# Self-attention of a decoder layer: mask and maxima in one VectorE instruction per head and row half

## The chip, the cores and the metric

The kernel runs on one core of one Trainium2 chip. The metric is the device time of one execution in microseconds (us). The core has a matrix engine (TensorE, PE in the profile, with its weight loads shown as PEld), a vector engine (VectorE, DVE), an activation engine (ScalarE, ACT), a general engine (GpSimd, POOL) and a queue engine (SyncE, SP), which all run their own instruction streams and wait for each other by semaphores.

## What is computed

One decoder layer on x of shape (16, 224, 512): causal self-attention with 16 heads of 32 channels, cross-attention to a context of 750 rows, and a gated recurrence with an output gate, each followed by a residual sum and a layer norm. Only the first of the three stages changes:

```python
def _L0_attn_ref(x, Wq, Wk, Wv, Wu, bu):          # h = 16 heads, c = 32
    xh = x.reshape(b, t, h, c)
    scale = d ** (-0.25)
    q = jnp.einsum('bthc,oc->btho', xh, Wq) * scale
    k = jnp.einsum('bthc,oc->btho', xh, Wk) * scale
    v = jnp.einsum('bthc,oc->btho', xh, Wv)
    scores = jnp.einsum('bihc,bjhc->bhij', q, k)
    scores = jnp.where(j > i, -jnp.inf, scores)
    attn = jax.nn.softmax(scores, axis=-1)
    y = jnp.einsum('bhij,bjhc->bihc', attn, v).reshape(b, t, d)
    return y @ Wu.T + bu
x = _layernorm(x + _L0_attn_ref(x, ...), axis=-1)
```

## The kernel before

Self-attention goes through 64 steps: step n is batch n // 4 and group g = n % 4 of four heads (G = 4). The 224 rows of a batch are two halves of R = 112 rows; the upper half (index 1, buffer `p1`, 224 columns) sees all columns up to its own, the lower half (index 0, buffer `p0`, 112 columns) only the first 112. Scores of head h stand in PSUM bank h (`ps_s`), first the upper half's 224 columns, then the lower half's 112. There is one set of these four banks, so the scores of step n+1 overwrite those of step n. The probabilities `p0` and `p1` have four buffers, one for each g.

The work is software-pipelined by hand: each engine has a function `steps` that lists, for step n, what it does for steps n, n-1, n-2, n-3 and n-4. An engine executes its list in order, so the order around the change is this.

- TensorE (`tensor`, L231 to L442), step n: `s(n)` the scores (L261), `t(n-2, 1)` a transposition of four 112x112 blocks (L292), `pv(n-3)` the products with the rows of x (L304, L307), `t(n-2, 2)`, `t(n-1, 0)`, in even steps `z` (the projected columns of a coming step, L243 to L247), and between them the pieces of the output projection `w` (L321), one of 128x512 each: seven in an odd step, five in an even one.
- ScalarE (`scalar`), step n: `exp(n)` for heads 0 and 1, `exp(n)` for heads 2 and 3 (L459; with the row sums through an accumulator, so each exponential is two instructions), `yh(n-3)` (L469) between or after them, `pt_copy(n-2)` (L485), and in even steps `open_projection` (L478) and `z_copy` (L492).
- VectorE (`vector`), step n: `inverse(n-1)` (the reciprocal of the row sums, L578), in even steps `yl(n-4)` (L591), `smax(n)` for heads 0 and 1 (L569 and L570: the negated maximum of the upper half and of the lower half), `pt_copy(n-2, 1)` (L585), `smax(n)` for heads 2 and 3, in even steps `yl(n-3)`, `norm` (L622) and `residual` (L599), in odd ones `statistics` (L605), in every fourth `moments` (L613, L615), and last `pt_copy(n-1, 0)` (L585).
- GpSimd (`gpsimd`), step n: `normalise(n-1)`, which multiplies `p1` and then `p0` by the reciprocals (L757), and in odd steps `query_parts` (L744, L746) for a coming `z`.

The causal mask is added by TensorE. `mask` is a bf16 tile of 0 and -1e30 for two identical triangles; one product of it with the bf16 identity (224 columns) puts it on the last 112 columns of the upper half and on the 112 columns of the lower half of one head. For heads 0 to 2 these products (L268) stand ahead of the score products and open the bank, each as soon as ScalarE has taken the exponentials of the same head of the step before; for head 3 it stands behind them (L279). The score products are L272 (224 columns) and L275 (112 columns). They wait until all exponentials of the step before are taken (`exp_done`), since ScalarE reads the scores in PSUM. `smax` waits for each head (`s_done`).

## Time and profile before

| | |
|---|---|
| median of 3 runs | 1409.38 us |
| the 3 runs | 1409.38, 4735.66, 1404.38 us |
| the profiled execution | 1403.68 us |
| its span (first to last instruction) | 1401.7 us |
| mean granted TensorE clock | 0.997 |
| self-attention in that span | from 0 to some 377 us |

The profile is one execution. Busy time is the union of an engine's instruction records; the records of neighbouring instructions overlap by some hundredths of a us, so the time that an instruction takes of its engine is read from the start of one to the start of the next. TensorE's records overlap more. [...]

### The profile page before, as it was taken

The numbers are of one execution on the slowest core, as the hardware profiler recorded it, in microseconds if no ns is written. First come the engines' busy times: TensorE is split into PE (matmuls) and PEld (weight loads), VectorE is DVE, ScalarE is ACT, GpSimd is POOL, SyncE is SP. The second block draws the span as 40 slices with busy tenths as digits, with TensorE's granted clock in tenths as the row PEclk, the third lists the DMA queues.
The fourth block names the chain that finished last, engine by engine and source line by source line (L and its number), as shares of the span: only waits on it lengthen the run. The fifth ranks groups of instructions, "written<-read, shape, count | busy, mean of one in ns | idle before, by whom it ended". The sixth has DMA issues, their size and how long they took to land.

```text
span 1401.7 us, 28348 instructions
## 1 busy us (share of the span) xinstructions
PE 1370.4 (98%) x9969; PEld 1203.7 (86%) x9969; DVE 862.9 (62%) x1911; ACT 731.7 (52%) x2005; POOL 574.7 (41%) x475
## 2 busy tenths in 40 slices
PE   7999999999989999999999999999999999999997
PEld 3677777777789999999999888999999999999775
DVE  4589989999745555654664372445443454536697
ACT  4588888888565566566656454222222222322232
POOL 2567767676556665656566520000000000010264
PEclk9999999999999999999999999999999999999999
DMA  6114323336288899889999963011010100000363
GB/s 215 38 44 107 105 77 80 105 103 170 80 216 184 215 221 218 188 220 210 208 199 226 214 177 102 0 27 27 0 26 0 26 13 20 31 1 31 105 188 121
DMA packets 141651, 159.07 MB, mean 113 GB/s; under 512 B 70400, under 2 KB 78592, under 8 KB 141568
## 3 DMA queue, kind: packets, MB, share of 16 engines
q1 hardware_dynamic: 133888, 157.96, 44.7%
q10 hardware_dynamic: 7680, 0.03, 0.4%
q8 instruction: 49, 0.80, 0.3%
q14 instruction: 34, 0.28, 0.1%
HBM read 106.57 MB, written 35.80 MB: 102 GB/s over the span
## 4 chain that ended last, share of the span: by engine, by line
PE 63%; issue 3%; DMA 3%; POOL 2%; DVE 1%; ACT 1%; POOLq 0%; SPq 0%; ACTq 0%; DVEq 0%
PE banks L1603 16%; PE banks L1632 11%; PE banks L1040 9%; PE banks L1056 8%; PE banks L1634 6%; PE banks L1025 5%; PE banks L1072 5%; DMA s_x1t<-x_halves 1%; POOL o_r L2178 1%; PE banks L1010 1%; PE banks L2064 1%; DMA x_halves<-s_ahead_halves 1%; PE banks L1088 1%; POOL o_rstd L2186 1%; PE banks L2095 0%
## 5 line engine op out<-in xcount | busy, mean ns | idle before, releaser
L459 ACT ACTIVATE s_p<-banks,a_nmax 112x224 f32<-112x224 f32 (+1 forms) x512 | 198.5, 413 | 58.4 <-DVE a_nmax L570 58.3
L757 POOL TENSOR_TENSOR s_p<-s_p,a_rinv 112x896 f32<-112x896 f32 (+1 forms) x128 | 164.7, 1308 | 116.9 <-DVE a_rinv L578 113.8
L1577 POOL CAST m_hi<-w_raw 128x2048 fp32r<-128x2048 f32 x1 | 2.3, 2265 | 407.7 <-PE banks L1603 407.7
L1720 ACT ACTIVATE f_gate<-f_gate 128x448 f32<-128x448 f32 x90 | 52.1, 579 | 198.7 <-DVE f_gate L1843 198.7
L1438 POOL TENSOR_TENSOR s_ct<-s_ct_raw,s_ct 128x750 fp32r<-128x750 f32 x60 | 108.3, 1835 | 111.5 <-ACT s_ct L1159 111.5
L1840 DVE TENSOR_TENSOR f_gate<-banks,f_xg_early 128x448 f32<-128x448 f32 x45 | 28.1, 624 | 189.6 <-PE banks L1634 189.6
L1445 POOL TENSOR_TENSOR x_cx_lo<-s_cx_raw,x_cx_hi 125x512 fp32r<-125x512 f32 x96 | 121.4, 1305 | 27.2 <-ACT x_cx_hi L1187 27.1
L569 DVE TENSOR_REDUCE a_nmax<-banks 112x1 f32<-112x224 f32 x256 | 97.7, 382 | 23.1 <-PE banks L275 22.4
L459 ACT ACTIVATION_READ_ACCUMULATOR s_p<-banks,a_nmax 112x1 f32 x512 | 111.8, 218 | 0.0
L292 PEld LDWEIGHTS banks<-identity,s_p 112*112 112x112 f32 x768 | 87.7, 134 | 21.6 <-issue 2.1
L292 PE MATMUL banks<-identity,s_p 112*112 112x112 f32 x768 | 105.0, 260 | 1.2 <-POOL s_p L757 0.7
L585 DVE COPY a_pt<-banks 112x448 f32<-112x448 f32 x128 | 78.7, 615 | 18.4 <-PE banks L292 18.3
L1056 PE MATMUL banks<-s_ct,x_zt_hi 128*112 128x376 f32 x480 | 86.9, 332 | 1.6 <-issue 1.6
L1320 DVE TENSOR_REDUCE x_smax<-banks 112x1 f32<-112x750 f32 x32 | 30.0, 938 | 90.3 <-PE banks L1056 90.3
L1056 PEld LDWEIGHTS banks<-s_ct,x_zt_hi 128*112 128x112 f32 x480 | 80.9, 175 | 1.9 <-issue 1.8
L1603 PE MATMUL banks<-s_xt,s_wc 128*128 128x448 f32 x360 | 75.4, 365 | 0.0
L1603 PE MATMUL banks<-s_xt,s_wi 128*128 128x448 f32 x360 | 75.3, 365 | 0.0
L1603 PEld LDWEIGHTS banks<-s_xt,s_wc 128*128 128x128 f32 x360 | 67.6, 188 | 5.3
L1603 PEld LDWEIGHTS banks<-s_xt,s_wi 128*128 128x128 f32 x360 | 67.6, 188 | 5.3
L570 DVE TENSOR_REDUCE a_nmax<-banks 112x1 f32<-112x112 f32 x256 | 67.2, 262 | 0.0
L1707 ACT ACTIVATE f_xg_late<-banks,bias 128x448 f32<-128x448 f32 x48 | 30.4, 634 | 69.1 <-PE banks L1603 69.1
L1180 ACT ACTIVATE x_ot_hi<-banks 128x448 fp32r<-128x448 f32 (+4 forms) x48 | 18.4, 419 | 91.1 <-PE banks L1040 91.1
(254 smaller groups left out, 3635.3 us busy)
## 6 DMA issues: line engine op xcount, KB each, us to landing
s_ct_raw<-in_ct SPq DMA_DIRECT2D x16, 1500.0 KB, 7.5
s_cx_raw<-in_cx SPq DMA_DIRECT2D x16, 1344.0 KB
a_xt<-in_xt SPq DMA_DIRECT2D x16, 448.0 KB, 6.4
a_xrow<-in_x SPq DMA_DIRECT2D x16, 448.0 KB, 5.8
a_xres<-in_x SPq DMA_DIRECT2D x16, 448.0 KB, 6.8
x_scratch<-a_xn SPq DMA_DIRECT2D x16, 448.0 KB, 3.3
out<-o_y SPq DMA_DIRECT2D x28, 256.0 KB, 2.0
s_ahead<-x_scratch SPq DMA_DIRECT2D x14, 448.0 KB
```

The source lines that it names most:

```text
L292: mm = pe.transpose(ps_t[0:R, (g + unit) % 2, h * R:h * R + R], src, identity[0:R, 0:R])
L459: e = act.activation((p1 if c else p0)[:, g, h, :], src, ACT.Exp, bias=nmax[:, g % 2, c, h:h + 1], accum_out=rsum[:, g % 2, c, h:h + 1])
L569: dve.tensor_reduce(nmax[:, g % 2, 1, h:h + 1], ps_s[0:R, h, 0:T], AX.X, ALU.max, negate=True)
L585: dve.tensor_copy(transposed(g, unit), unit_bank(g, unit)).then_inc(ptd_done, 1)
L757: pool.tensor_tensor(p[:, g, :, :], p[:, g, :, :], inv, ALU.mult).then_inc(norm_done, 1)
L1040: mm = pe.matmul(pair(ps_g, dk), v[:, j, 128 * dk:128 * dk + 128], q[:, j, :], start=(i == 0), stop=(i == 3 * XC - 1))
L1056: mm = pe.matmul(ps_s[0:R, 2 * c + half, 0:XH + 1], z[:, k, c * R:c * R + R], x[:, k, half * XH:half * XH + XH + 1], start=(i == 0), stop= ...
L1438: low = pool.tensor_tensor(ct_lo[:, k, 0:TX], ct_raw[:, k, :], ct_hi[:, k, 0:TX], ALU.subtract)
L1445: pool.tensor_tensor(cx_lo[:, j, :], cx_raw[:, j, :], cx_hi[:, j, :], ALU.subtract).then_inc(cxl_done, 1)
L1603: mm = pe.matmul(ps_x[:, t % 2, 0:2 * T], w["w" + n][wp][:, k, m], xp[:, k, :, :], start=(i == 0), stop=(i == 3 * KC - 1))
L1632: pe.matmul(ps_gate[:, 2 * j + k2, 0:2 * T], hi[:, k, m], cc[:, k, :, :], start=(k == 0), stop=False, skip_group_check=True)
L1634: mm = pe.matmul(ps_gate[:, 2 * j + k2, 0:T], lo[:, k, m], cc[:, k, 0, :], start=False, stop=(k == KC - 1), skip_group_check=True)
```

## The change

- The mask products L268 and L279, the bf16 identity and the bf16 mask are gone from TensorE. `s(n)` is four products of 224 columns and four of 112.
- `smax` becomes `masked_max`: for each head and each half one `tensor_tensor_reduce` on VectorE. It reads the scores from PSUM and an fp32 mask from SBUF, writes -(score + mask) as fp32 into `p1` or `p0`, and gives the minimum over the row, which is the negated maximum, through VectorE's accumulator.
- `exp` reads `p1` or `p0` in SBUF and writes it in place, with scale -1.0; it does not read PSUM.
- `s(n)` waits for the maxima of step n-1 (`max_done`), not for its exponentials.
- The wait for the scores stands in front of the reciprocal: `inverse(n-1)` waits until all four heads' scores of step n are done, and for the transpositions that free the `p` buffers. The waits by head in `smax` and ScalarE's wait for the transpositions are gone.
- On GpSimd the mask is built in fp32 and the copy of the identity to bf16 is gone. `spacer` takes the room of the removed tiles.

```diff
--- before.py
+++ after.py
@@ -57,8 +57,7 @@
             return ctx.enter_context(nc.semaphore("a_" + name))
 
         identity = shared.identity
-        identity_b = sb("identity_b", [R, R], BF16)
-        mask = sb("mask", [R, 2, R], BF16)
+        spacer = sb("spacer", [R, 340], BF16)
         wq4 = sb("wq4", [C, G, C])
         wk4 = sb("wk4", [C, G, C])
         a_diag = sb("a_diag", [128, 128])
@@ -95,6 +94,7 @@
         ones = sb("ones", [128, R])
         bq = sb("bq", [128, KC, 1])
         bk = sb("bk", [128, KC, 1])
+        mask = sb("mask", [R, 2, R])
 
         const_ready = sem("const_ready")
         bias_in = sem("bias_in")
@@ -144,6 +144,7 @@
         def transposed(g, unit):
             return (pt0[:, g % 2, :, R:T], pt1[:, g % 2, :, :], pt0[:, g % 2, :, 0:R])[unit]
 
+        MOST = 3.0e38
         ZBIAS, ZBIAS_PART = (3, 4), {3: (0, 1), 4: (2, 3)}
         ZB, QK = 2 * T, 2 * T + 8
         WU, KB, MP = 0, KC, KC + 1
@@ -262,22 +263,14 @@
                 if not within(n, STEPS):
                     return
                 wait(pe, zc_done, m + 1)
-                last = G - 1
-                for h in range(last):
-                    wait(pe, exp_done, G * (n - 1) + h + 1)
-                    pe.matmul(ps_s[0:R, h, R:T + R], identity_b[:], mask[:, :, :], start=True, stop=False, skip_group_check=True)
-                wait(pe, exp_done, G * n)
+                wait(pe, max_done, G * n)
                 for h in range(G):
                     rows = slice(C * h, C * h + C)
-                    pe.matmul(ps_s[0:R, h, 0:T], zs[rows, g, R:T], xt[rows, odd, g, :], start=(h == last), stop=False, skip_group_check=True)
+                    pe.matmul(ps_s[0:R, h, 0:T], zs[rows, g, R:T], xt[rows, odd, g, :], start=True, stop=False, skip_group_check=True)
                 for h in range(G):
                     rows = slice(C * h, C * h + C)
-                    mm = pe.matmul(ps_s[0:R, h, T:T + R], zs[rows, g, 0:R], xt[rows, odd, g, 0:R], start=False, stop=(h < last),
-                                   skip_group_check=True)
-                    if h < last:
-                        mm.then_inc(s_done, 1)
-                pe.matmul(ps_s[0:R, last, R:T + R], identity_b[:], mask[:, :, :], start=False, stop=True,
-                          skip_group_check=True).then_inc(s_done, 1)
+                    pe.matmul(ps_s[0:R, h, T:T + R], zs[rows, g, 0:R], xt[rows, odd, g, 0:R], start=False, stop=True,
+                              skip_group_check=True).then_inc(s_done, 1)
 
             def t(n, g, unit):
                 if not within(n, STEPS):
@@ -399,7 +392,7 @@
 
             pe.wait_ge(prep_act, 1)
             z(0, 0, 0, 1)
-            pe.wait_ge(const_ready, 8)
+            pe.wait_ge(const_ready, 7)
 
             def steps(i, odd):
                 b = 2 * i + odd
@@ -451,12 +444,11 @@
             def exp(n, g, heads):
                 if not within(n, STEPS):
                     return
-                wait(act, t_done, 3 * (n - 3))
                 for h in heads:
                     wait(act, max_done, G * n + h + 1)
                     for c in (1, 0):
-                        src = ps_s[0:R, h, 0:T] if c else ps_s[0:R, h, T:T + R]
-                        e = act.activation((p1 if c else p0)[:, g, h, :], src, ACT.Exp, bias=nmax[:, g % 2, c, h:h + 1],
+                        p = (p1 if c else p0)[:, g, h, :]
+                        e = act.activation(p, p, ACT.Exp, scale=-1.0, bias=nmax[:, g % 2, c, h:h + 1],
                                            accum_out=rsum[:, g % 2, c, h:h + 1])
                     e.then_inc(exp_done, 1)
 
@@ -561,18 +553,26 @@
             first_z()
 
         def vector(dve):
-            def smax(n, g, heads):
+            def masked_max(n, g, heads):
+
                 if not within(n, STEPS):
                     return
+                if isinstance(n, int) and n == 0:
+                    dve.wait_ge(s_done, G)
                 for h in heads:
-                    wait(dve, s_done, G * n + h + 1)
-                    dve.tensor_reduce(nmax[:, g % 2, 1, h:h + 1], ps_s[0:R, h, 0:T], AX.X, ALU.max, negate=True)
-                    dve.tensor_reduce(nmax[:, g % 2, 0, h:h + 1], ps_s[0:R, h, T:T + R], AX.X, ALU.max, negate=True)\
+                    dve.tensor_tensor_reduce(out=p1[:, g, h, :], in0=ps_s[0:R, h, 0:T], in1=mask[:, :, :].rearrange("p a t -> p (a t)"),
+                                             scale=-1.0, scalar=MOST, op0=ALU.add, op1=ALU.min, accum_out=nmax[:, g % 2, 1, h:h + 1])
+                    dve.tensor_tensor_reduce(out=p0[:, g, h, :], in0=ps_s[0:R, h, T:T + R], in1=mask[:, 1, :],
+                                             scale=-1.0, scalar=MOST, op0=ALU.add, op1=ALU.min, accum_out=nmax[:, g % 2, 0, h:h + 1])\
                        .then_inc(max_done, 1)
 
             def inverse(n, g):
+
                 if not within(n, STEPS):
                     return
+                if within(n + 1, STEPS):
+                    wait(dve, t_done, 3 * (n - 2))
+                    wait(dve, s_done, G * (n + 2))
                 wait(dve, exp_done, G * (n + 1))
                 wait(dve, norm_done, 2 * (n - 1))
                 dve.reciprocal(rinv[:, g % 2, :, :], rsum[:, g % 2, :, :]).then_inc(rinv_done, 1)
@@ -621,7 +621,7 @@
                 wait(dve, stored, 16 * b)
                 dve.tensor_scalar(xn[:, c, :], r[:, c, :], mv[:, c, 0:1], rstd[:, c, :], ALU.subtract, ALU.mult).then_inc(xn_done, 1)
 
-            dve.wait_ge(const_ready, 9)
+            dve.wait_ge(const_ready, 8)
             dve.wait_ge(bias_in, 32)
             for k in range(KC):
                 dve.tensor_scalar(bk_all[:, k, :], ones[:], bk[:, k, :], None, ALU.mult).then_inc(spread, 1)
@@ -686,9 +686,9 @@
                     inverse(n - 1, (g - 1) % NG)
                     if g % 2 == 0 and not (isinstance(n, int) and n == STEPS + 2):
                         yl(n - 4, g, 1 - odd)
-                    smax(n, g, (0, 1))
+                    masked_max(n, g, (0, 1))
                     pt_copy(n - 2, (g - 2) % NG, 1)
-                    smax(n, g, (2, 3))
+                    masked_max(n, g, (2, 3))
                     if g % 2 == 0:
                         yl(n - 3, (g - 3) % NG, y_odd)
                     if isinstance(n, int):
@@ -722,12 +722,10 @@
             pool.wait_ge(const_ready, 5)
             pool.affine_select(out=identity[:], in_=identity[:], compare_op=ALU.is_equal, fill=0.0, base=0,
                                pattern=[[-1, 128]], channel_multiplier=1).then_inc(const_ready, 1)
-            pool.affine_select(out=mask[:], in_=mask[:], compare_op=ALU.is_ge, fill=NEG, base=0,
-                               pattern=[[0, 2], [-1, R]], channel_multiplier=1).then_inc(const_ready, 1)
-            pool.wait_ge(const_ready, 7)
-            pool.tensor_copy(identity_b[:], identity[0:R, 0:R]).then_inc(const_ready, 1)
+            pool.affine_select(out=mask[:, 1, :], in_=mask[:, 1, :], compare_op=ALU.is_ge, fill=NEG, base=0,
+                               pattern=[[-1, R]], channel_multiplier=1).then_inc(const_ready, 1)
             pool.memset(ones[:], 1.0).then_inc(const_ready, 1)
-            pool.wait_ge(const_ready, 9)
+            pool.wait_ge(const_ready, 8)
 
             def early(n):
```

## Rows read from the trace of the kernel before

**Rows 1.** The page: the span, and the busy time of each engine.

```profile
span 1401.7 us, 28348 instructions
PE 1370.4 (98%) x9969; PEld 1203.7 (86%) x9969; DVE 862.9 (62%) x1911; ACT 731.7 (52%) x2005; POOL 574.7 (41%) x475
```

**Rows 2.** Busy time by stretch: start:end, length, PE, PEld, DVE, ACT, POOL, clock, DMA.

```profile
80.34:343.58 263.24, 263.24 (x2887) 198.86 (x2887) 238.68 (x742) 225.32 (x989) 184.01 (x167) 1.00 0.37 98
```

**Rows 3.** TensorE in order of time, one odd step: start, length, line, count.

```profile
257.57 0.65 PE L272 MATMUL banks<-a_xt,a_zs 32*112 32x224 f32 x8
...
258.34 0.30 PE L279 MATMUL banks<-a_mask,a_identity_b 112*112 112x224 bf16 x1
258.41 0.46 PE L321 MATMUL banks<-a_w_hi,a_yt_hi 128*112 128x512 f32 x1
...
262.16 0.45 PE L268 MATMUL banks<-a_mask,a_identity_b 112*112 112x224 bf16 x3
262.54 0.65 PE L272 MATMUL banks<-a_xt,a_zs 32*112 32x224 f32 x8
```

**Rows 4.** Who waited for whom, 80.34 to 343.58 us: us in total, times, longest.

```profile
POOL s_p L757 <- DVE a_rinv L578: 70.7, 39, 3.0
ACT s_p L459 <- DVE a_nmax L570: 37.9, 52, 1.2
DVE a_nmax L569 <- PE banks L275: 16.1, 40, 0.7
```

**Rows 5.** VectorE in order of time, the second half of an even step.

```profile
254.78 0.38 DVE L569 TENSOR_REDUCE a_nmax<-banks 112x1 f32<-112x224 f32 x1
255.08 0.26 DVE L570 TENSOR_REDUCE a_nmax<-banks 112x1 f32<-112x112 f32 x1
255.26 0.38 DVE L569 TENSOR_REDUCE a_nmax<-banks 112x1 f32<-112x224 f32 x1
...
256.75 0.69 DVE L599 TENSOR_TENSOR a_r<-banks,a_xres 112x512 f32<-112x512 f32 x1
257.36 0.61 DVE L585 COPY a_pt<-banks 112x448 f32<-112x448 f32 x1
257.89 0.19 DVE L578 RECIPROCAL a_rinv<-a_rsum 112x8 f32<-112x8 f32 x1
258.43 0.39 DVE L569 TENSOR_REDUCE a_nmax<-banks 112x1 f32<-112x224 f32 x1 [0.35 <-PE banks L275]
```

**Rows 6.** VectorE, the same kind of instruction elsewhere, with no GpSimd work beside it.

```profile
363.78 0.68 DVE L660 CUSTOM_DVE_ANT_0 s_dot<-s_x_raw,s_kbias 112x512 f32<-112x512 f32 x1
364.39 0.08 DVE L660 DVE_READ_ACCUMULATOR2_ANT s_rowdot<- 112x1 f32 x1
364.51 0.69 DVE L660 CUSTOM_DVE_ANT_0 s_dot<-s_x_raw,s_kbias 112x512 f32<-112x512 f32 x1
```

**Rows 7.** VectorE and then GpSimd in cross-attention, where both work.

```profile
419.14 0.08 DVE L1285 DVE_READ_ACCUMULATOR2_ANT s_rowdot<- 112x1 f32 x1
419.25 2.17 DVE L1285 CUSTOM_DVE_ANT_0 s_dot<-s_ahead,s_kbias 112x512 f32<-112x512 f32 x1
...
418.56 6.02 POOL L1438 TENSOR_TENSOR s_ct<-s_ct_raw,s_ct 128x750 fp32r<-128x750 f32 x3 [6.75 <-ACT s_ct L1159]
```

**Rows 8.** One line of VectorE, all its instructions: min/median/max ns.

```profile
L591 DVE TENSOR_TENSOR a_yt_lo<-banks,a_yt_hi x64: 331/386/392, 37.5 to 365.4; 128x224 fp32r<-128x224 f32 x64
```

**Rows 9.** ScalarE in order of time.

```profile
257.16 0.59 ACT L485 ACTIVATE a_pt<-banks 112x448 f32<-112x448 f32 x1
257.58 0.66 ACT L478 ACTIVATE banks<-a_bu_all 112x512 f32<-112x512 f32 x1
258.10 0.60 ACT L492 ACTIVATE a_zs<-banks 128x448 f32<-128x448 f32 x1
```

**Rows 10.** GpSimd in order of time, beside rows 3 and 5.

```profile
258.16 2.57 POOL L757 TENSOR_TENSOR s_p<-s_p,a_rinv 112x896 f32<-112x896 f32 x2 [2.26 <-DVE a_rinv L578]
```

## The prediction

> **What bounds the kernel now.** I read the page first: TensorE is busy for 98% of the span and no other engine for more than 62% [rows 1]. That is a mean over three stages, so I then asked for busy time by stretch, inside self-attention alone. From 80.34 to 343.58 us, in 263.24 us, L279 runs 52 times, once a step: the period is 263.24 / 52 = 5.06 us. In that stretch TensorE is busy all the time at the granted clock 1.00, VectorE 238.68 us, ScalarE 225.32 us and GpSimd 184.01 us [rows 2]; per step that is 5.06, 4.59, 4.33 and 3.54 us. So TensorE sets the pace, but VectorE is only half a microsecond behind it. The waits say the same: VectorE waits for the scores (16.1 us over 40 waits), ScalarE waits for the maxima of VectorE (37.9 us, 0.73 us a step) and GpSimd for the reciprocal (70.7 us) [rows 4]; TensorE has no such wait. A step that takes work from TensorE can win only what VectorE leaves free, and this one gives work to VectorE.
>
> **What it takes from TensorE.** Four mask products a step. The three of L268 start at 262.16 and L272 of the next step at 262.54: 0.38 us. The one of L279 takes 0.07 us, from 258.34 to 258.41 [rows 3]. Together 0.45 us: TensorE needs 5.06 - 0.45 = 4.61 us a step. Some 56 of the 64 steps run at the pace of 5.06 us (from 65 to 349 us), so that this relief alone is worth at most 56 x 0.45 = 25 us, and 64 x 0.45 = 29 us if the eight slower first steps gained it too.
>
> **What it gives to VectorE.** First its load now. 4.59 us is the union of the records, and a record reaches 0.08 us into the next one: `smax` on 224 columns is 0.38 us long and the next starts after 0.30 us [rows 5]. Only ahead of an idle stretch does this tail count as busy without holding anything; with one or two such stretches a step the true load is 4.59 - 0.1 = 4.49 us.
>
> The eight main instructions. `smax` takes 0.30 us for 224 columns (254.78 to 255.08) and 0.18 us for 112 (255.08 to 255.26) [rows 5]: 1.07 ns for each column and 0.06 us besides. The new instruction reads a second tensor and writes a row. The same kind of instruction, with 512 columns, goes from 363.78 to 364.39, 0.61 us [rows 6], as long as L599 with one PSUM and one SBUF input, 256.75 to 257.36 [rows 5]. Taking off 288 columns leaves 0.30 us for 224. So the main instruction costs what `smax` costs, at most 0.01 us more: I put 8 x 0.01 = 0.08 us a step.
>
> The eight accumulator reads are new: `smax` has none, while the instruction at L660 is followed by one, 0.08 us long [rows 6]. How long it holds the engine is the number on which this case hangs, and no row shows it freely. From the start of the read at 364.39 to the next instruction at 364.51 it is 0.12 us, but that one waits for the read by a semaphore, so 0.12 us is the upper bound. The lower bound is 0 (an added instruction gives nothing back): it would vanish in the tail of the main one. I take 0.07 us, since the nearest row without a wait is the 0.06 us that any VectorE instruction costs beside its columns. Eight reads are 0.56 us.
>
> [...]
>
> VectorE then needs 4.49 + 0.08 + 0.56 = 5.13 us a step. It passes TensorE's 4.61 us and becomes the bound.
>
> **Waits that move.** The scores of step n+1 wait for the maxima of step n, not for its exponentials. That is earlier by a whole exponential pass, and no row shows TensorE waiting there in steady state, so it gains nothing. But it is what lets TensorE run ahead once it has slack: its scores start right after the last `masked_max` (3.3 us into VectorE's even step) and take 0.77 us (257.57 to 258.34, rows 3), so they are done at about 4.2 us, and VectorE asks for them at 5.1 to 5.5 us. Now they come late: the reciprocal at 257.89 is followed by 0.35 us idle until the scores of one head stand [rows 5]. The new wait for all four heads, ahead of the reciprocal, has behind it the reciprocal, for which GpSimd waits, and the whole step of VectorE; in an odd step without `moments`, which has only 4.3 us of work, it is met with nearly no slack. I put 0.03 us a step for that and for the exponentials, which end at about the same moment.
>
> ScalarE reads `p` in SBUF instead of PSUM. L478, SBUF input, takes 0.52 us for 512 columns (257.58 to 258.10), L485, PSUM input, 0.42 us for 448 [rows 9]. At most 0.10 us more for each of eight exponentials, more likely half of it as 64 columns have their part: 4.33 + 0.4 = 4.7 us, under 5.1 even where both ends are added (5.13). It is hidden behind VectorE; if VectorE were as quick as TensorE, ScalarE would cost up to 0.1 us a step. The wait for transpositions goes from ScalarE to VectorE and was met three steps ago. The mask in fp32 is 224 columns made once, and the copy of the identity goes: nothing, as VectorE starts only when the biases land.
>
> **The sum.** 5.13 + 0.03 = 5.16 us a step against 5.06: 56 x 0.10 = 5.6 us, and 0.5 us for the first and last steps, where masks and reads stand in a chain. Against the profiled execution (span 1401.7, time 1403.7 us) that is 1403.7 + 6 = 1410 us. The profiled time is near the lowest of the three runs, so 1410 is on that scale and not 1409.4 + 6. Two per cent of it, about what a measurement of this kernel can tell from no change, is 28 us or 0.5 us a step.
>
> **Rivals.**
> The reads are nearly free (0 to 0.03 us). VectorE needs 4.57 to 4.81 us and the pace is 4.61 to 4.84 us. Gain 56 x 0.22 to 0.45 = 12 to 25 us, so 1379 to 1391 us, say 1385. For it: reads are 0.08 us long and the tail that records share is 0.08 us. Against it: every instruction seen holds its engine for 0.06 us at least.
>
> The reads hold the engine until the value is written (0.12 us). VectorE needs 4.49 + 0.08 + 0.96 + 0.03 = 5.56 us: + 28 us, 1432 us. This ends on the other side: from 0.06 us a read on, (5.06 - 4.57 - 0.03) / 8, the kernel is slower than before. For it: it is the only number that a row shows. Against it: that row has a wait.
>
> The new wait costs turns. If the wait for four heads made VectorE and TensorE alternate, the idle 0.35 us of rows 5 would stay on top of VectorE's load, say 0.3 us a step: 56 x 0.4 = 22 us, 1426 us. Against it is the 1 us by which the scores come early.
>
> GpSimd stops VectorE. In cross-attention the same instruction took 2.17 us instead of 0.68, and ended only after a GpSimd instruction had ended [rows 7]. In self-attention GpSimd starts 2.57 us of products over `p` just after each reciprocal [rows 10], beside the masked maxima. If these were stopped until the first of the two had ended, that is 1.4 us a step or more: + 80 us, some 1490 us. Against it: the stopped instruction had both inputs in SBUF, and the new one has one in PSUM, like L591, whose 64 instances never took more than 392 ns while GpSimd worked [rows 8].
> [...]
>
> **Chances.** Forecast 0.55, reads free 0.15, reads at full length 0.17, turns 0.08, GpSimd 0.05. The 80% range runs from 1388 (a read of 0.02 to 0.03 us) to 1436 us (0.12 us a read and some stall); it leaves out GpSimd and the ends of the others. Faster by over 2% needs reads at nothing and the first steps too: 0.04. Slower by over 2%: GpSimd, and somewhat under half of the full-length case and of turns: 0.14. The rest, 0.82, is within 2%.
>
> **What would show it.** In the changed profile VectorE is busy for nearly all of the stretch from 80 to 345 us, with some 5.1 us a step, TensorE shows gaps of half a microsecond a step ahead of the scores, released by VectorE, and `max_done`'s waiter is TensorE. The start of a read to the next main instruction is 0.06 to 0.08 us; at 0.03 or 0.12 the second or third case holds. Main instructions are 0.38 and 0.27 us long; 1 us or more among them means GpSimd. An idle VectorE ahead of the reciprocal, released by L275's successor, means turns. The forecast is wrong if the period is under 5.0 or over 5.4 us.

## The result and the profile after

| | before | after |
|---|---|---|
| median, runs of this comparison | 1407.56 us, 4 runs | 1423.07 us, 4 runs |
| the profiled execution | 1403.68 us | 1422.56 us |
| its span | 1401.7 us | 1420.8 us |
| ratio of the medians, see below | | 1.012, 95% interval 1.0099 to 1.0141 |
| one step of self-attention | 5.06 us | 5.33 us |
| first score product of cross-attention starts at | 376.86 us | 394.40 us |

The change makes the kernel 1.2% slower. One of the four runs before took 4735.66 us; the median in the table counts it, the ratio doesn't, and is 1423.07 over the 1405.74 us of the other three. The time lies in the forecast range, the sign is the forecast's, but the loss is 19 us in the profiled executions where 6 us were forecast, and it comes from somewhere else than the forecast said.

The first thing to read is the page of totals, the counterpart of [rows 1].

```profile
span 1420.8 us, 28089 instructions
PE 1362.4 (96%) x9713; PEld 1182.2 (83%) x9713; DVE 870.2 (61%) x2423; ACT 749.2 (53%) x2005; POOL 575.0 (40%) x474
```

TensorE has lost its mask products and is at 96%. The next view is busy time by stretch, over 48 steps of self-attention (columns: start and end, length, busy time and instructions of PE, PEld, DVE, ACT and POOL, granted TensorE clock, DMA share, GB/s). It answers to [rows 2].

```profile
87.85:343.54 255.69, 233.65 (x2477) 164.74 (x2472) 229.85 (x1068) 221.27 (x913) 171.49 (x156) 1.00 0.32 83
```

255.69 / 48 = 5.33 us a step. TensorE is busy for 4.87 us of them, VectorE for 4.79, ScalarE for 4.61: **no engine is the bound any more.** The forecast said that VectorE would be busy nearly throughout, at 5.1 us a step. In such a picture busy shares have no more to say; what is wanted is who waits for whom. The waits of the same stretch (engine, tile and line that waited, who released it: us in total, times, longest), against [rows 4]:

```profile
POOL s_p L755 <- DVE a_rinv L578: 79.1, 42, 2.9
ACT s_p L451 <- DVE a_nmax L565: 32.6, 24, 1.5
DVE a_rinv L578 <- PE banks L272: 16.7, 41, 0.8
...
PE banks L314 <- ACT banks L470: 11.5, 24, 0.6
...
PE banks L244 <- DVE a_yt_lo L591: 9.2, 20, 0.5
```

VectorE now waits for all four heads' scores (L272) with its reciprocal: 16.7 / 48 = 0.35 us a step. Once in two steps TensorE waits for ScalarE's `open_projection` (L470) and, nearly as often, `z` waits for VectorE's `yl` (L591). Each waits for another: a ring. It can be followed. The next three fences are timelines of VectorE, TensorE and ScalarE (start, length, instruction, and in brackets the idle time before it and who ended it).

```profile
253.59 0.21 DVE L578 RECIPROCAL a_rinv<-a_rsum 112x8 f32<-112x8 f32 x1 [0.81 <-PE banks L272]
253.72 0.34 DVE L591 TENSOR_TENSOR a_yt_lo<-banks,a_yt_hi 128x224 fp32r<-128x224 f32 x1
253.97 0.38 DVE L563 CUSTOM_DVE_ANT_0 s_p<-banks,a_mask 112x224 f32<-112x224 f32 x1
254.28 0.08 DVE L563 DVE_READ_ACCUMULATOR2_ANT a_nmax<- 112x1 f32 x1
254.28 0.27 DVE L565 CUSTOM_DVE_ANT_0 s_p<-banks,a_mask 112x112 f32<-112x112 f32 x1
254.47 0.09 DVE L565 DVE_READ_ACCUMULATOR2_ANT a_nmax<- 112x1 f32 x1
254.47 0.39 DVE L563 CUSTOM_DVE_ANT_0 s_p<-banks,a_mask 112x224 f32<-112x224 f32 x1
```

```profile
248.66 0.48 PE L314 MATMUL banks<-a_w_hi,a_yt_hi 128*112 128x512 f32 x1 [0.43 <-ACT banks L470]
...
252.52 0.65 PE L269 MATMUL banks<-a_xt,a_zs 32*112 32x224 f32 x8
252.99 0.37 PE L272 MATMUL banks<-a_xt,a_zs 32*112 32x112 f32 x8
...
259.25 0.49 PE L314 MATMUL banks<-a_w_hi,a_yt_hi 128*112 128x512 f32 x1 [0.43 <-ACT banks L470]
```

```profile
248.02 0.58 ACT L470 ACTIVATE banks<-a_bu_all 112x512 f32<-112x512 f32 x1
...
254.59 0.48 ACT L451 ACTIVATE s_p<-s_p,a_nmax 112x224 f32<-112x224 f32 x1 [1.31 <-DVE a_nmax L565]
254.98 0.19 ACT L451 ACTIVATION_READ_ACCUMULATOR s_p<-s_p,a_nmax 112x1 f32 x1
255.07 0.37 ACT L451 ACTIVATE s_p<-s_p,a_nmax 112x112 f32<-112x112 f32 x1
...
258.19 0.52 ACT L477 ACTIVATE a_pt<-banks 112x448 f32<-112x448 f32 x1
258.62 0.58 ACT L470 ACTIVATE banks<-a_bu_all 112x512 f32<-112x512 f32 x1
```

The chain: `open_projection` starts at 248.02 and releases the first projection piece of the odd step on TensorE (248.66, after 0.43 us idle). TensorE executes its list, and the last score product starts at 252.99. That releases VectorE's reciprocal (253.59, after 0.81 us idle), behind which stand `yl` and the first masked maxima. Those release ScalarE's exponentials (254.59, after 1.31 us idle), behind which stand `pt_copy` (258.19) and `open_projection` (258.62), and the round begins again. The pieces are 0.64 + 4.33 + 0.60 + 1.00 + 3.60 + 0.43 = 10.60 us, which is two steps. (The mean of two steps is 10.65 us: every second pair has `moments` in VectorE's list and takes some 10.7 us. There VectorE's own work stands where the 0.81 us of idle time stand here.) So the pace is the length of a ring through three engines. An edit that lengthens a piece of it costs time though every engine has room, and one that shortens an engine's load elsewhere gives nothing.

### The profile page after: what moved, and what is told of

It is laid out like the page before. It is cut to its first block, busy times and chain, and to the rows that moved or that the text cites. A ratio compares the mean times of both kernels' runs of the same rounds, so it can differ in the third digit from the quotient of the medians.

```text
span 1420.8 us, 28089 instructions
## 1 busy us (share of the span) xinstructions
PE 1362.4 (96%) x9713; PEld 1182.2 (83%) x9713; DVE 870.2 (61%) x2423; ACT 749.2 (53%) x2005; POOL 575.0 (40%) x474
## 4 chain that ended last, share of the span: by engine, by line
PE 61%; issue 3%; DMA 3%; POOL 2%; DVE 1%; ACT 1%; SPq 0%; POOLq 0%; ACTq 0%; DVEq 0%
PE banks L1601 15%; PE banks L1630 10%; PE banks L1038 8%; PE banks L1054 8%; PE banks L1632 6%; PE banks L1023 5%; PE banks L1070 5%; DMA s_x1t<-x_halves 1%; POOL o_r L2176 1%; PE banks L1008 1%; DMA x_halves<-s_ahead_halves 1%; PE banks L1086 1%; POOL o_rstd L2184 1%; PE banks L2062 1%; PE banks L2093 0%
## 5 line engine op out<-in xcount | busy, mean ns | idle before, releaser
L451 ACT ACTIVATE s_p<-s_p,a_nmax 112x224 f32<-112x224 f32 (+1 forms) x512 | 215.7, 423 | 58.8 <-DVE a_nmax L565 56.9
L285 PE MATMUL banks<-identity,s_p 112*112 112x112 f32 x768 | 105.8, 261 | 1.6 <-POOL s_p L755 1.4
L285 PEld LDWEIGHTS banks<-identity,s_p 112*112 112x112 f32 x768 | 87.3, 134 | 23.6 <-POOL s_p L755 2.7
L563 DVE CUSTOM_DVE_ANT_0 s_p<-banks,a_mask 112x224 f32<-112x224 f32 x256 | 96.9, 379 | 0.0
L451 ACT ACTIVATION_READ_ACCUMULATOR s_p<-s_p,a_nmax 112x1 f32 x512 | 96.0, 187 | 0.0
L585 DVE COPY a_pt<-banks 112x448 f32<-112x448 f32 x128 | 79.3, 620 | 19.1 <-PE banks L285 18.9
L314 PE MATMUL banks<-a_w_hi,a_yt_hi 128*112 128x512 f32 x128 | 59.4, 472 | 16.4 <-ACT banks L470 16.3
L565 DVE CUSTOM_DVE_ANT_0 s_p<-banks,a_mask 112x112 f32<-112x112 f32 x256 | 69.0, 269 | 0.0
```

Of the source, the lines that this page charges most:

```text
L285: mm = pe.transpose(ps_t[0:R, (g + unit) % 2, h * R:h * R + R], src, identity[0:R, 0:R])
L451: e = act.activation(p, p, ACT.Exp, scale=-1.0, bias=nmax[:, g % 2, c, h:h + 1], accum_out=rsum[:, g % 2, c, h:h + 1])
L563: dve.tensor_tensor_reduce(out=p1[:, g, h, :], in0=ps_s[0:R, h, 0:T], in1=mask[:, :, :].rearrange("p a t -> p (a t)"), scale=-1.0, scalar= ...
L585: dve.tensor_copy(transposed(g, unit), unit_bank(g, unit)).then_inc(ptd_done, 1)
```

## The experiments

The pace below is read from busy time by stretch, each over 48 steps, as above; "start of cross-attention" is where its first score product stands. In each comparison the kernel before was run again on the same chip; there its median was between 1406.7 and 1412.8 us, so a ratio goes with its own comparison and the times of different rows are not to be set against each other to the microsecond.

| run | us a step | start of cross-attention | time, median | ratio to before, 95% |
|---|---|---|---|---|
| before | 5.062 | 376.86 | 1407.56 | 1 |
| after | 5.327 | 394.40 | 1423.07 | 1.012 (1.0099 to 1.0141) |
| e1_late_wait | 5.096 | 382.21 | 1410.14 | 1.0025 (1.0011 to 1.0039) |
| e2_open_first | 5.293 | 391.15 | 1423.14 | 1.0118 (1.0086 to 1.0149) |
| e3_both | 5.078 | 379.84 | 1407.20 | 1.0005 (0.9991 to 1.0019) |
| e4_before_wait_four | 5.452 | 398.78 | 1427.3 | 1.0165 (1.0138 to 1.0192) |
| e5_before_no_mask | 4.929 | 368.96 | 1407.24 | 1.000 (0.9974 to 1.0026) |
| e6_psum_in_place | 5.158 | 386.31 | 1416.38 | 1.0058 (1.0036 to 1.0080) |
| e7_psum_open_first | 5.163 | 386.57 | 1417.47 | 1.0078 (1.0054 to 1.0103) |
| e8_before_wait_one | 5.255 | 388.00 | 1421.85 | 1.0109 (1.0086 to 1.0133) |
| e9_late_wait_turn_first | 4.982 | 373.03 | 1405.4 | 0.995 (0.9925 to 0.9976) |
| e10_before_turn_first | 5.055 | 374.87 | 1412.13 | 1.0001 (0.998 to 1.0023) |
| e11_after_turn_first | 5.170 | 381.93 | 1419.61 | 1.0042 (1.0016 to 1.0068) |

### The wait, later: e1_late_wait

The changed kernel with its two new waits, for the scores and for the transpositions, moved from ahead of the reciprocal to ahead of the first masked maximum. They are carried by a two-element `memset`, which also takes the place of the one wait ahead of step 0.

```diff
 def inverse(n, g):
-    if within(n + 1, STEPS):
-        wait(dve, t_done, 3 * (n - 2))
-        wait(dve, s_done, G * (n + 2))
     wait(dve, exp_done, G * (n + 1))
...
     yl(n - 4, g, 1 - odd)
+    if within(n, STEPS):
+        wait(dve, t_done, 3 * (n - 3))
+        wait(dve, s_done, G * (n + 1))
+        dve.memset(spacer[:, 0:2], 0.0)
     masked_max(n, g, (0, 1))
```

> The changed kernel, with VectorE's wait for the four heads' scores moved from in front of the reciprocal to behind the reciprocal and yl(n-4), on a one-column memset. Theory A (a ring of waits sets the pace: open_projection, the odd TensorE step, the scores, reciprocal, yl and first maximum, eight exponentials, pt_copy, open_projection, 10.68 us for two steps): the reciprocal and yl leave the ring, 0.38 us, the memset enters, some 0.07 us, so 10.37 us for two steps and 28 x 0.31 = 9 us less: about 1414 us. Theory B (VectorE's load sets the pace): the load grows by the memset, so no change or up to 3 us more, 1423 to 1426 us.

Measured: 1410.14 us, 0.9% under the changed kernel, and 5.10 us a step instead of 5.33. But for the `memset`, all work is the same. First the stretch of 48 steps, then the step that answers to the one followed above (an even one without `moments` ahead of it): VectorE's three instructions, and TensorE's last score products.

```profile
93.38:338.00 244.62, 232.63 (x2473) 164.68 (x2472) 227.58 (x1116) 221.25 (x914) 171.17 (x156) 1.00 0.33 88
```

```profile
246.43 0.19 DVE L573 RECIPROCAL a_rinv<-a_rsum 112x8 f32<-112x8 f32 x1
246.54 0.36 DVE L586 TENSOR_TENSOR a_yt_lo<-banks,a_yt_hi 128x224 fp32r<-128x224 f32 x1
247.24 0.39 DVE L561 CUSTOM_DVE_ANT_0 s_p<-banks,a_mask 112x224 f32<-112x224 f32 x1 [0.33 <-issue]
```

```profile
246.71 0.37 PE L272 MATMUL banks<-a_xt,a_zs 32*112 32x112 f32 x8
```

The reciprocal now starts 0.28 us ahead of the last score products (246.43 and 246.71), and `yl` behind it. VectorE is still idle, for 0.33 us and no longer 0.81, but with both of them done. The first maximum starts 0.53 us after the last score products do, where it was 0.98 us (252.99 to 253.97). The rest of the round is the same: TensorE still waits for `open_projection` 25 times in the stretch.

What follows: 0.23 us a step of the new kernel's 5.33 are the place of these waits. The run moves the wait for the transpositions too, but the profile of the changed kernel names the scores (L272) as what ended the idle time, and e4 below has that wait alone. That VectorE's load, nearly unchanged (4.74 us against 4.79), sets the pace is refuted.

### Another order on ScalarE: e2_open_first and e3_both

e2 is the changed kernel with `open_projection` ahead of `pt_copy` in even steps, e3 is that with e1's late wait.

```diff
+if g == 0:
+    open_projection(b - 2, 1)
+if g == 2:
+    open_projection(b - 1, 0)
 pt_copy(n - 2, (g - 2) % NG)
...
 if g == 0:
-    open_projection(b - 2, 1)
     z_copy(2 * b + 1, 1)
 if g == 2:
-    open_projection(b - 1, 0)
     z_copy(2 * b + 2, 0)
```

> The changed kernel, with ScalarE's open_projection moved ahead of pt_copy in even steps. Theory A: pt_copy, 0.42 us from start to start, leaves the ring of two steps: 28 x 0.42 = 12 us less, about 1411 us. Theory B: VectorE's work is the same, no change, 1423 us.

> Both edits, the wait behind the reciprocal and yl and open_projection ahead of pt_copy. Theory A: 0.31 + 0.42 = 0.73 us less for two steps unless another wait ends last, 28 x 0.73 = 20 us less, about 1403 us. Theory B: 1423 to 1426 us.

e2 gains nothing to be seen: 1423.14 against 1423.07 us, 5.29 us a step. Theory A, the ring, had expected 12 us less, so it was wrong here. The waits of the stretch show why:

```profile
PEld banks L285 <- issue: 8.2, 25, 0.4
...
PE banks L314 <- ACT banks L470: 3.6, 16, 0.3
```

TensorE's wait for `open_projection` (L314) fell from 11.5 to 3.6 us, and its transpositions (L285) wait for `pt_copy`, which now is the later of the two. The profile calls this wait "issue"; that it is `pt_copy` is read from the times (one `pt_copy` starts at 257.59 and is 0.53 us long, and the weight loads of L285 start at 258.23 after 0.35 us idle) and from e9 below, where the profile names that releaser. Two instructions of ScalarE release two of TensorE that stand side by side; to swap them swaps the wait. The ring as followed above had left this second wait out. In e3, with the late wait, the swap gains 0.018 us a step, and the time is that of before (1.0005).

### The wait alone, in the kernel before: e4_before_wait_four and e8_before_wait_one

The other way round: the kernel before, with nothing but the wait ahead of the reciprocal. e4 waits for four heads, e8 for the first only.

```diff
 def inverse(n, g):
+    if within(n + 1, STEPS):
+        wait(dve, s_done, G * (n + 2))        # e8: G * (n + 1) + 1
     wait(dve, exp_done, G * (n + 1))
```

> The kernel before, with one wait added: the reciprocal of step n-1 waits until all four heads' scores of step n stand. Nothing else changes. Theory A: reciprocal and yl (0.38 us) and the three later heads with the last mask product (0.25 us) enter a ring that had some 0.17 us of slack in 10.12 us: + 0.46 us for two steps, 28 x 0.46 = 13 us more than before, about 1420 us, so three quarters of the change's loss. Theory B: VectorE keeps its half a microsecond of slack a step and TensorE stays the bound, no change, 1407 us.

> The kernel before, with the reciprocal of step n-1 waiting for the scores of the first head of step n alone. With the wait for all four heads two steps went from 10.12 to 10.91 us, 0.79 us more. If the order (reciprocal and yl behind the scores) is what costs, three other heads and the last mask product give back 0.25 to 0.3 us and 0.5 us stay: 28 x 0.5 = 14 us over before, about 1421 us. If waiting for all four heads is what costs, this one is within 5 us of before, 1407 to 1412 us.

Stretch of 48 steps of e4, its reciprocal in VectorE's timeline, and the same kind of step in the kernel before:

```profile
92.23:353.93 261.70, 251.88 (x2666) 185.52 (x2665) 225.93 (x685) 207.97 (x914) 170.97 (x157) 1.00 0.31 83
```

```profile
257.14 0.20 DVE L580 RECIPROCAL a_rinv<-a_rsum 112x8 f32<-112x8 f32 x1 [1.34 <-PE banks L279]
```

```profile
262.43 0.19 DVE L578 RECIPROCAL a_rinv<-a_rsum 112x8 f32<-112x8 f32 x1
262.54 0.34 DVE L591 TENSOR_TENSOR a_yt_lo<-banks,a_yt_hi 128x224 fp32r<-128x224 f32 x1
263.40 0.39 DVE L569 TENSOR_REDUCE a_nmax<-banks 112x1 f32<-112x224 f32 x1 [0.52 <-PE banks L275]
```

The wait alone costs more than the whole change: 5.45 us a step, 1.65% of the time (1427.3 us, where theory A had 1420 and theory B no loss). In the kernel before, 0.52 us of idle time stand behind the reciprocal and `yl`; with the wait, 1.34 us stand ahead of them. In the stretch from 92 to 343 us these are 29.6 us over 35 waits. e8 divides the cost: to wait for one head before the reciprocal is + 0.19 us a step (order alone), for the other three and the fourth head's mask product another 0.20. The changed kernel pays 0.27 us and not 0.39. It also has a TensorE list without the masks' 0.45 us, scores that don't wait for the exponentials, and longer exponentials; no run parts these three.

### The relief alone: e5_before_no_mask

The kernel before without its mask products; the mask is left out of the computation. Each head's first score product opens its bank, and its last one signals `s_done`.

```diff
 for h in range(last):
     wait(pe, exp_done, G * (n - 1) + h + 1)
-    pe.matmul(ps_s[0:R, h, R:T + R], identity_b[:], mask[:, :, :], start=True, stop=False, skip_group_check=True)
...
-pe.matmul(ps_s[0:R, last, R:T + R], identity_b[:], mask[:, :, :], start=False, stop=True,
-          skip_group_check=True).then_inc(s_done, 1)
```

> The kernel before without the mask products L268 and L279; its scores are not masked, nothing stands in their place. It shows what the relief of TensorE alone is worth. Theory A (waits in a ring): TensorE needs 4.61 us a step and the ring loses the 0.38 us of L268 once in two steps, from 9.95 to 9.6 us, so TensorE's 9.2 us or the ring's 9.6 us for two steps bounds it: 28 x 0.5 to 0.9 = 14 to 25 us less than before, 1382 to 1393 us. Theory B (VectorE's load of 4.49 us is near the pace too): the pace stops at 4.6 us, 1382 us.

Its stretch of 48 steps, its largest new wait, and the same wait in the kernel before, over the same 255.69 us:

```profile
89.07:325.67 236.60, 231.15 (x2472) 164.72 (x2473) 222.04 (x684) 207.97 (x914) 170.89 (x156) 1.00 0.35 92
```

```profile
PEld banks L271 <- ACT s_p L454: 17.3, 40, 0.5
```

```profile
PEld banks L272 <- ACT s_p L459: 0.8, 5, 0.2
```

0.45 us of products go from an engine that was busy for 100% of the time, and the pace falls by 0.13 us, from 5.06 to 4.93. The rest meets a wait that was hardly there before (0.8 us over 5 waits): the scores of a step wait for the exponentials of the last one, 17.3 us in 255.69 us, some 52 of its steps, or 0.33 us a step. It is a wait of the weight load ahead of the products, and about what is missing of the relief (0.45 - 0.13 = 0.32 us): the mask products had filled that time. So the relief alone, in the kernel before, is 0.13 us and not the 0.45 us that were forecast as its most. Both of the expected figures, 1382 to 1393 us, were wrong.

Cross-attention started 7.9 us earlier, and yet the median is that of before, 1407.24 us. In its profiled execution the part from step 63 of self-attention to the end takes 1064.2 us, against 1053.1 before. One thing to be seen there is TensorE's granted clock, which falls to 0.50 for some us each at about 409, 583 and 785 us. This is the stretch around the second of them:

```profile
580.00:590.00 10.00, 7.31 (x51) 7.32 (x52) 5.36 (x8) 4.62 (x7) 3.27 (x2) 0.83 0.55 128
```

TensorE was busy for 73% of it. In the profiled execution of the kernel before the clock fell, to 0.50 as well, only at about 47 us and over the last 6 us. That remainder, whose code is nearly the same in all kernels, moves from one to the next, and it goes with the clock. It is shortest in the two profiled executions whose clock doesn't fall between step 63 and the last few us, 1053.1 us in the kernel before and 1052.5 in e4. In the eleven others it falls there one to three times, and the remainder is 1055.4 (e9) to 1064.2 us (e5): 1057.7 in the changed kernel, 1059.6 in e1, 1063.2 in e10. The ten executions of e5 say the same: the three with a mean granted clock of 0.994 took 1402.4 to 1404.6 us, the four with 0.990 or less 1412.8 to 1413.3 us. The falls alone can't be all of it: in e5's profiled execution they last 10 us together, and at a granted clock of 0.50 that is at most some 5 of the 11 us. Whether TensorE ran short of work first and the clock fell for it, and why that comes more often in e5, stays open. For the reader of such tables it means that some us of a kernel's time can come from behind the edited part, and the pace is the better measure of the edit.

### The masked scores in PSUM: e6_psum_in_place and e7_psum_open_first

These test what the exponentials' SBUF input costs. e6 is e1 with the masked scores written back to their PSUM bank, read there by the exponentials; the scores must then wait for `exp_done`. e7 is the same of e3.

```diff
-wait(pe, max_done, G * n)
+wait(pe, exp_done, G * n)
...
-dve.tensor_tensor_reduce(out=p1[:, g, h, :], in0=ps_s[0:R, h, 0:T], ...)
+dve.tensor_tensor_reduce(out=ps_s[0:R, h, 0:T], in0=ps_s[0:R, h, 0:T], ...)
...
-e = act.activation(p, p, ACT.Exp, scale=-1.0, ...)
+e = act.activation(p, src, ACT.Exp, scale=-1.0, ...)      # src: the scores in PSUM
```

> The first experiment (wait behind the reciprocal and yl), with the masked scores written back in place to PSUM; the exponentials read PSUM as before the change, and the scores of the next step wait for the exponentials again. Theory A with ScalarE's pass in the ring: each exponential is 0.04 us shorter from PSUM, 8 a step, so the ring of 10.19 us for two steps loses 0.34 us, unless the scores now wait for the last exponential: 28 x 0.34 = 9 us less than the first experiment, about 1400 us. If the SBUF source costs nothing on the path: 1410 us as in the first experiment, or more by the wait for exponentials.

> The same with open_projection ahead of pt_copy. It was worth 0.04 us for two steps beside the late wait, as pt_copy then ended last in place of it. With ScalarE's pass shorter: the same 1 to 3 us less than without it, about 1398 us; below the kernel before (1407 us) by 9 us. If TensorE's z and w pieces bound it by then, no difference to the kernel without it.

Both are worse than what they were made from: 5.16 us a step, 1416 and 1417 us against 1410 and 1407, where 1400 and 1398 us were expected. The waits of e6:

```profile
PEld banks L269 <- ACT s_p L452: 20.6, 40, 0.8
...
PE banks L269 <- ACT s_p L452: 6.4, 28, 0.4
```

The wait of e5 is back, and longer. ScalarE got its 0.23 us a step back (210.26 us busy in the 48 steps against 221.25 in e1) and it was of no use. VectorE became slower too: a masked maximum of 112 columns that writes to PSUM takes 0.232 us to the next instruction, where it took 0.194 with SBUF as its output, half of those of 224 columns take 0.35 us where they took 0.31, and VectorE's busy time rises from 227.58 to 234.47 us in the 48 steps, 0.14 us a step:

```profile
255.12 0.32 DVE L564 CUSTOM_DVE_ANT_0 banks<-banks,a_mask 112x112 f32<-112x112 f32 x1
...
255.35 0.43 DVE L562 CUSTOM_DVE_ANT_0 banks<-banks,a_mask 112x224 f32<-112x224 f32 x1
...
255.70 0.32 DVE L564 CUSTOM_DVE_ANT_0 banks<-banks,a_mask 112x112 f32<-112x112 f32 x1
```

So e6 changes three things at once: the exponentials' input, the maxima's output and what the scores wait for. It doesn't price the SBUF input. That letting the scores wait for the maxima, and not for the exponentials, is worth something is likely from the wait that is back here and stood in e5, but it isn't shown alone.

### TensorE's transposition ahead of a projection piece: e9, e10, e11

In e1 the projection piece behind the scores is one of those that wait for ScalarE, and a transposition, which VectorE waits for, stands behind it. e9 is e1 with the two swapped, e10 is the kernel before and e11 the changed kernel with the same swap.

```diff
 s(n, 2 * b + g // 2, odd, g)
-w(0, 1)
 t(n - 2, (g - 2) % NG, 1)
+w(0, 1)
 w(1, 2)
```

> The first experiment (wait behind the reciprocal and yl) with TensorE's order changed: the transposition t(n-2, 1) goes ahead of the first piece of the output projection, so that it runs while ScalarE still writes open_projection. Theory A (the ring through ScalarE's pass and open_projection): 0.3 us of transpositions leave the ring of 10.19 us for two steps, so 28 x 0.3 = 8 us less than the first experiment, about 1402 us, below the kernel before. If the ring was not what held the first experiment at 5.10 us a step, 1410 us.

> The kernel before with the same order of TensorE alone. There the first piece did not wait for open_projection, so by theory A nothing leaves the path: within 2 us of before, 1405 to 1409 us. If the order itself is worth something without the change: 1399 us.

> The changed kernel, wait in its place ahead of the reciprocal, with the same order of TensorE. Theory A: the ring of 10.65 us for two steps loses 0.3 us: 8 us less than the changed kernel, about 1415 us. If VectorE's load or the wait alone sets the pace: 1423 us.

e9, stretch of 48 steps and its longest wait of TensorE itself:

```profile
90.36:329.49 239.13, 230.34 (x2474) 160.22 (x2473) 228.60 (x1118) 220.29 (x915) 170.97 (x157) 1.00 0.34 91
```

```profile
PE banks L285 <- ACT a_pt L477: 8.7, 26, 0.5
```

4.98 us a step, and 1405.4 us against 1412.82 of the kernel before on the same chip: 0.995, interval 0.9925 to 0.9976. It is the only version faster than before. Of the 7.4 us between the medians, the start of cross-attention accounts for 3.8 us (376.86 - 373.03, in two profiled executions). The swap gives 0.11 us a step to e1 and 0.16 to the changed kernel (e11, 5.17 us), and next to nothing to the kernel before (e10, 5.06 us), where theory A had 0.15, 0.15 and nothing. In the kernel before TensorE had no such wait to be covered. With the wait late and this order, the change is a small gain: 0.08 us a step. This is the test of the ring that came out about as expected: what takes work out from behind `open_projection` shortens the step, and only where TensorE waits for it.

## Why the prediction was right and wrong

**Direction and size.** 1410 us was forecast in a range from 1388 to 1436; the median is 1423.07. By its own scale, the profiled execution, the forecast was + 6 us and the measurement + 19 us. Of 19.1 us of span, 17.5 us (394.40 - 376.86) lie ahead of cross-attention, 1.6 us behind. The 56 steps at full pace hold 56 x 0.265 = 14.8 of them, the first and last steps 2.7 us, where 0.5 us were forecast. That the sign and the range came out is luck: the forecast had 0.56 us a step for accumulator reads that cost nothing, and 0.03 us for the wait that made the loss.

**"The eight accumulator reads": 8 x 0.07 us a step, measured 0.** The forecast called this the number on which the case hangs. In the timeline above the read at L563 starts at 254.28, and so does the next main instruction; 254.47 again. A main instruction takes 0.31 us (224 columns) and 0.19 to 0.20 us (112) to the next one, with the read in between, against 0.30 and 0.18 of `smax` [rows 5]. So the forecast's main instruction, at most 0.01 us above `smax`, is right, and with it the reads hold nothing. The lower bound, "it would vanish in the tail of the main one", is what happened. The 0.12 us of [rows 6] were the wait. The choice of 0.07 was drawn from "the 0.06 us that any VectorE instruction costs beside its columns", and the reads cost nothing of the kind: from the start of one to the start of the next instruction it is 0.00 us for all 188 of L563 between 92 and 343 us. The timeline shows the overlap: the read starts at 254.28, while the record of its main instruction goes on to 254.35.

**"VectorE ... passes TensorE's 4.61 us and becomes the bound": wrong.** VectorE is busy for 4.79 us a step of 5.33 and idle for the rest; without the reads its forecast load was 4.57. Two of the signs that were named as proof did not come: it is not busy throughout, and the start of a read to the next main instruction is neither 0.06 nor 0.08.

**The rival "reads nearly free" had the reads right and the time wrong**, 1385 us. Its pace, 4.61 to 4.84 us, takes what the fullest engine needs for the pace, as the forecast does. No run comes to 4.61 us: without the mask products, and with nothing added, it is 4.93 us (e5). That isn't TensorE's need in the changed kernel, since e5 keeps a wait for exponentials that the change takes away; whether "TensorE needs 5.06 - 0.45 = 4.61 us" is right stays open. What e5 refutes is that the relief comes back as pace wherever the next engine leaves room. The sentence "no row shows TensorE waiting there in steady state" was true and misread: no wait shows where some other work lies in its time, and that work was the mask products themselves. The union of overlapping records called TensorE 100% busy, which left no room for this.

**"I put 0.03 us a step" for the new wait: the step that failed most.** Moving it, with the one for the transpositions, gives 0.23 us a step back (e1); adding only that wait to the kernel before costs 0.39 (e4). What it rested on, that the scores are done at about 4.2 us of VectorE's step and asked for at 5.1 to 5.5, supposed that TensorE runs ahead once it has slack. It doesn't: it waits for `open_projection`, that for the exponentials, and those for the maxima behind this very wait. The rival "the new wait costs turns" had the mechanism, its sign ("an idle VectorE ahead of the reciprocal", now 0.35 us a step) and the time (1426 us, measured 1423.07), and got 0.08 of the chance. The forecast's own bound, wrong under 5.0 or over 5.4 us, could not tell the two apart at 5.33. The rival's sum had the idle time on top of a VectorE load of 5.1 us; the measured one is a ring in which no engine is full. The argument against it, "the 1 us by which the scores come early", was computed from starts that the change itself moves.

**ScalarE's SBUF input: size right, "hidden" not shown.** An exponential of 224 columns takes 0.373 us to the next instruction and was 0.330, one of 112 columns 0.279 and was 0.237: + 0.043 us each, 0.34 us a step, inside the forecast's 0.4. The load is 4.61 us against 4.7 forecast. The forecast hid this behind VectorE. It lies in the ring's piece of 3.60 us, so it is not covered by a full engine; what it costs there no run shows, since e6, made for it, changed two other things.

**GpSimd doesn't stop VectorE.** This rival is out: L563's 192 instances in the stretch have a mean of 379 ns, the forecast's 0.38 us, beside 171 us of GpSimd's work on SBUF:

```profile
L563 DVE CUSTOM_DVE_ANT_0 s_p<-banks,a_mask 112x224 f32<-112x224 f32 x192 | 72.7, 379 | 0.0
```

**"`max_done`'s waiter is TensorE"**, with gaps ahead of the scores: wrong. TensorE's largest gap is ahead of the first projection piece, and what releases it is ScalarE.

## What to carry to other kernels

When three engines alternate in a fixed order, write down the round (who releases whom, until you are back at the start) and its length before you price an edit by engine loads; here the pace was that round over its steps, 5.33 us, and not the fullest engine's 4.87. A wait for "all of it" is set down as late in an engine's list as the data is needed: instructions that don't need it, above all those that others wait for, go ahead of it; here that place was worth 0.23 us a step. Compare the same kind of step when two timelines are laid side by side: here the steps differ by `yl` and `moments`, and a gap of 0.81 us in one is none in the next but one. And work that looks like pure cost may stand in time that would be a wait without it, so the worth of its removal has to be measured alone: here 0.13 us a step, where 0.45 us of work were taken out.

## What the runs showed of the hardware

- An accumulator read behind a reducing VectorE instruction, 0.08 us long, starts together with the next instruction and costs 0.00 us from start to start, where nothing waits for it (all 188 reads of L563 between 92 and 343 us). ScalarE's is different: the next exponential starts 0.09 us after the read (254.98 to 255.07).
- The masked maximum with one PSUM and one SBUF input and an SBUF output takes 0.01 us longer than the plain maximum from PSUM (0.31 and 0.194 us to the next instruction, against 0.30 and 0.181). With its output in PSUM (e6) the one of 112 columns takes 0.232 us.
- ScalarE's exponential takes some 0.043 us more from SBUF than from PSUM, the same for 112 and 224 columns (0.279 against 0.237 us, 0.373 against 0.330); with the changed kernel's scale and PSUM as its source (e6) it takes 0.24 and 0.33 again.
- TensorE at "100% busy" by the union of its records was not simply full: 0.45 us of products a step were taken out in e5, and 0.13 us came back, because a wait of the next weight load stood behind them (17.3 us over 40 waits, 0.33 us a step, and 0.8 us over 5 in the kernel before).
- In eleven of the thirteen profiled executions the granted TensorE clock fell between the scores of self-attention's last step and the last few us, at places that differ from kernel to kernel. In the changed kernel this one has a mean of 0.91:

```profile
420.00:440.00 20.00, 18.03 (x109) 17.07 (x108) 10.98 (x16) 13.29 (x23) 12.86 (x9) 0.91 0.92 243
```

TensorE was busy for 18.03 of the 20 us there. In the kernel before it was busy for all 20.00 us of the same stretch, at 1.00, with DMA at a share of 0.81. What set it off was not tried.
